# Second attention of a fused block on one core: rotation at later heads, score matmuls for one head at a time

## What is computed

```python
q, k, v = (proj(Wq), proj(Wk), proj(Wv))            # (b, H, s, d)
q, k = _rope(q, k, s, d, hidden_states.dtype)       # q*cos + _rotate_half(q)*sin, the same for k
scores = einsum('bhqd,bhkd->bhqk', q, k) / sqrt(d)
scores = maximum(scores + causal, neg)
tmp_sum = sum(softmax(scores, axis=-1), axis=-2)    # column sums
_, topk_idx = top_k(tmp_sum, int(0.1 * s))          # heavy columns
mask = heavy_mask[:, :, None, :] | band             # band: |i - j| <= 25
scores = where(mask, scores, neg)
attn = einsum('bhqk,bhkd->bhqd', softmax(scores, axis=-1), v)
return attn @ Wo.T
```

## Time and profile before

| | us |
|---|---|
| median of 3 runs | 2262.65 (2259.99 to 2265.01) |
| profiled execution | 2258.55 |
| its span in the trace | 2256.7 |
| PE, PEld busy | 2000.1, 1674.2 |
| DVE, ACT, POOL busy | 1312.0, 930.6, 219.9 |

### The profile page before, as it was taken

How to read it: one execution, slowest core, us unless ns; L and a number is a source line. 1 busy time by engine, 2 the same in 40 slices (tenths; PEclk the granted TensorE clock), 3 DMA queues, 4 the chain that set the end, 5 groups by cost and what they waited for, 6 DMA issues and landing times.

```text
span 2256.7 us, 84567 instructions
## 1 busy us (share of the span) xinstructions
PE 2000.1 (89%) x34605; PEld 1674.2 (74%) x34605; DVE 1312.0 (58%) x4974; ACT 930.6 (41%) x3362; POOL 219.9 (10%) x338
## 2 busy tenths in 40 slices
PE   5788888888889798866799999998999999999999
PEld 3455565565555677666789898998898988988987
DVE  3456465565576049755666666665666666666653
ACT  2253443543555122233444444443444444444432
POOL 0011011011011100000011011010110110110112
PEclk9789888899798898966899999999999999999999
DMA  6100000000000561200000000000000000000000
GB/s 248 31 6 16 19 6 15 16 10 15 17 8 2 194 231 56 88 3 17 18 17 4 27 18 18 13 18 19 27 4 18 27 4 27 18 18 13 4 12 10
DMA packets 61862, 74.95 MB, mean 33 GB/s; under 512 B 8480, under 2 KB 49888, under 8 KB 60608
## 3 DMA queue, kind: packets, MB, share of 16 engines
q1 hardware_dynamic: 59024, 54.82, 7.9%
q0 software_dynamic: 2448, 14.68, 1.9%
HBM read 44.27 MB, written 16.81 MB: 27 GB/s over the span
## 4 chain that ended last, share of the span: by engine, by line
PE 50%; DVE 5%; issue 2%; ACT 1%; DMA 0%; DVEq 0%; POOL 0%; ACTq 0%
PE ps L1374 26%; PE ps L1328 11%; PE ps L1308 10%; PE ps L1362 2%; PE ps L1317 1%; DVE hbuf L1544 1%; DVE dh L1532 1%; DVE dh L1538 1%; DVE cn L1522 0%; ACT nn L1441 0%; DVE hbuf L1541 0%; DVE cn L1510 0%; DVE hn L1525 0%; DVE h L1542 0%; DVE ns L1534 0%
## 5 line engine op out<-in xcount | busy, mean ns | idle before, releaser
L1374 PE MATMUL ps<-hbuf,whf 128*128 128x32 f16 x24480 | 657.9, 177 | 81.6 <-DVE hbuf L1544 59.0
L1374 PEld LDWEIGHTS ps<-hbuf,whf 128*128 128x128 f16 x24480 | 647.8, 96 | 104.2 <-DVE hbuf L1544 61.7
L1421 ACT ACTIVATE rz<-s,sc 128x32 f32<-128x32 f32 x512 | 164.5, 321 | 522.5 <-DVE s L1510 511.2
L1308 PE MATMUL ps<-hbuf,w1f 128*128 128x256 f16 x2304 | 292.7, 274 | 0.0
L1328 PE MATMUL ps<-hh,w2f 128*128 128x256 f16 x2304 | 292.1, 275 | 0.0
L1510 DVE TENSOR_REDUCE s<-ps 128x32 f32<-128x64 f32 x512 | 114.8, 224 | 273.4 <-PE ps L1374 260.0
L1497 POOL TENSOR_TENSOR hh<-tb,hh 128x256 f16<-128x256 f32 x192 | 132.4, 695 | 1302.1 <-ACT hh L1468 1302.1
L1308 PEld LDWEIGHTS ps<-hbuf,w1f 128*128 128x128 f16 x2304 | 224.1, 98 | 32.2 <-issue 6.0
L1328 PEld LDWEIGHTS ps<-hh,w2f 128*128 128x128 f16 x2304 | 211.4, 98 | 44.5 <-issue 19.9
L640 ACT ACTIVATE E<-ps,nm 128x128 f32<-128x128 f32 x256 | 94.9, 371 | 255.1 <-DVE nm L712 253.7
L1018 PE MATMUL ps<-x1T,wi 128*128 x768 | 173.9, 389 | 19.8 <-DMA wi<-in_W_ih 13.7
(11 more groups left out here) (192 smaller groups left out, 2824.6 us busy)
## 6 DMA issues: line engine op xcount, KB each, us to landing
gi_d<-stage SPq DMA_DIRECT2D x96, 128.0 KB, 1.7
gi<-gi_d SPq DMA_DIRECT2D x16, 768.0 KB, 5.1
swp<-raw SPq DMA_DIRECT2D x256, 32.0 KB, 1.9
w1f<-in_w1T POOLq DMA_DIRECT2D x4, 1408.0 KB, 9.0
xall<-in_x SPq DMA_DIRECT2D x4, 1024.0 KB, 9.0
x1T<-in_xT SPq DMA_DIRECT2D x1, 4096.0 KB, 22.0
w2f<-in_w2T POOLq DMA_DIRECT2D x2, 2048.0 KB, 10.5
out<-x1T SPq DMA_DIRECT2D x8, 512.0 KB, 3.1
```

The costliest lines, as they stand in the source:

```text
L1308: last = nc.tensor.matmul(ps[:, 6 + i % 2, 0:TT], w[:, wp, e % EH, c * P:(c + 1) * P], hbuf[par][:, k, hq, :, :].rearrange("p s b -> p (s ...
L1374: last = nc.tensor.matmul(ps[:, bank, g * WIDE * 2 * B:(g + 1) * WIDE * 2 * B], whp[:, k, w, q, g * P:(g + 1) * P], h[:, k, :, :].unsqueez ...
L1421: nc.scalar.activation(rz[:, q, :, :].rearrange("p g b -> p (g b)"), s1[:, q, :, :].rearrange("p g b -> p (g b)"), ACT.Sigmoid, scale=sc[: ...
```

## The change

The score matmuls are issued for one head at each head, and not for two at every other head; their wait for a free bank is written for one head (h - 4 where it was h - 3). The slots of the rotation are later by 3 for the first two units, by 5 for the third (which moves to round 1) and by 2 for the fourth. In batch 0 the swap of unit 1 is issued by ACT, between its second and its third copy; SP issues the other three.

```diff
@@ -406,24 +406,26 @@
+        def swap(queue, b, u):
+
+            i, p = UNITS[u]
+            x = raw[:, b % 2, i, 2 * p:2 * p + 2, :]
+            queue.wait_ge(a_raw, b * NU + u + 1)
+            passed(queue, v_rot, (b * NU + u - 1) * 3)
+            half = DH2 // 2
+            for to in range(0, P, half):
+                of = to + half if to % DH2 == 0 else to - half
+                queue.dma_start(swp[to:to + half, u % 2, :, :], x[of:of + half, :, :]).then_inc(d_swap[u % 2], 16)
...
-                for b in range(B):
+                swap(sp, 0, 0)
+                swap(sp, 0, 2)
+                swap(sp, 0, 3)
+                for b in range(1, B):
                     for u in range(NU):
-                        swap(b, u)
+                        swap(sp, b, u)
@@ -451,12 +453,12 @@
                     n = b * (2 * NH) + r * NH + h
-                    passed(pe, a_e, (n + 1 - 4 + 1) * 2)
+                    passed(pe, a_e, (n - 4 + 1) * 2)
...
-                    pair = [(g, g % 4, g // HPC, slice(g % HPC * DH2, (g % HPC + 1) * DH2)) for g in (h, h + 1)]
-                    for g, bank, m, rows in pair:
+                    heads = [(g, g % 4, g // HPC, slice(g % HPC * DH2, (g % HPC + 1) * DH2)) for g in (h,)]
+                    for g, bank, m, rows in heads:
...
@@ -574,8 +576,7 @@
                     for h in range(NH):
-                        if h % 2 == 0:
-                            scores(b, 0, h)
+                        scores(b, 0, h)
@@ -606,8 +607,7 @@
                     for h in range(NH):
-                        if h % 2 == 0:
-                            scores(b, 1, h)
+                        scores(b, 1, h)
@@ -671,6 +671,8 @@
                 for u in range(NU):
                     copy_raw(0, u, 4 + u)
+                    if u == 1:
+                        swap(act, 0, u)
@@ -831,7 +833,7 @@
-ROTATE_AT = (4, 5, 6, 7, 8, 9, 12, 13, 14, NH + 8, NH + 9, NH + 10)
+ROTATE_AT = (7, 8, 9, 10, 11, 12, NH + 1, NH + 2, NH + 3, NH + 10, NH + 11, NH + 12)
```

## The result

| | before | after |
|---|---|---|
| median, us | 2263.83 (2259.99 to 2267.33, 4 runs) | 2290.16 (2282.57 to 2293.45, 4 runs) |
| profiled execution, us | 2258.55 | 2282.57 |
| its span | 2256.7 | 2280.7 |

The ratio of the times is 1.0112, with a 95% interval of 1.0081 to 1.0143: the change makes the kernel slower by 1.1%, 26 us. The forecast was 2284 us, 21 more than before.

The account below looks back on a forecast made before the run. The second attention was taken as PE-bound, losing time to waits and half-speed clock. Start 0, middle cycles -7, last batch +14 and +14 made +21 us: median 2262.65 to 2284 us, range 2240 to 2320.

Parts of the forecast that it names:

- The cost of a single head: Score matmuls: without overlap two single heads cost 0.95 us more than a pair, 122 us of PE work, 15.2 a cycle.
- The rotation: Second attention: later slots remove almost all 14.0 us of DVE swap waits and 9.4 us of PE waits in a cycle.
- The middle cycles: Six cycles between heavy-column copies: 84.5 us each against 85.6, -7 for the six; 81.1 each without low clock.
- the third: Middle cycles: share of the earlier low clock assumed to stay, 8% of the time at 1.2 GHz.
- The start: Start and batch 0: DVE begins about 3 us earlier, against 7.6 us for eight pairs, over half taken up by waits; sum 0.
- The last batch: Last batch, no projections: +14 us for the stretch through its round 0, and +14 for round 1 at low clock.
- the term of 6.8 us: Round 0 of the last batch: heads 4 to 11 run at 1.2 GHz until the output projections, costing 6.8 us.
- The part behind the stage: Everything after the second attention: forecast change 0.
- A: Rival: PE, busy with hardly a gap, stays at 2.4 GHz throughout; -26 us, 2236; chance 0.15.
- B: Rival: clock falls in middle batches at heads 5 to 7 of round 0 and stays low; +32, 2316; chance 0.18.
- C: Rival: single heads still overlap, half of the 0.95 us paid; about -40 on the forecast, near 2244; chance 0.05.
- D: Rival: rotation still waits for swaps, 1 to 2 us a batch; within 5 us of forecast; forecast with D 0.57.

Follow-up runs that it names:

- products by head: Pairs with late rotation, each pair's products issued one head then the other, masks of both still ahead, against the kernel before: 2176.76 us, ratio 0.9624.
- wide fill: Changed kernel plus six useless full-width fp32 matmuls at each of heads 0 to 2, round 1, last batch: 2264.01 us, ratio 0.9992 to the kernel before.
- the first two experiments: Changed kernel with scores in pairs again, late rotation: 2179.64 us, ratio 0.9642; changed kernel with early rotation slots, single heads: 2329.85 us, ratio 1.0275.
- the narrow fill: Changed kernel plus four useless 32-row fp32 matmuls at each of heads 0 to 2, round 1, last batch: 2299.89 us, ratio 1.0159 to the kernel before.

## Why the prediction was right, and where it was not

The direction and the mechanism were right: twice the time for the products of two heads, the waits of DVE gone, a last round at 1.2 GHz. That the sum came so close was in part luck. Of its terms the start missed by -7.0 us, round 0 of the last batch and what stands ahead of it by -4.3, the last round by +5.7 and the part behind the stage by +7.8, and these cancel but for 2 us.

**The cost of a single head** was right. A head of round 0 takes 1.05 us (1.06 forecast), one of round 1 at 1.2 GHz 2.25 (2.25 forecast). The upper bound, no overlap at all, was the right one to take. PE's busy time in the stage grew by 95 us (578.1 to 673.3), over 80 as forecast. The experiment with products by head adds what the trace of before could not show: the order of the products does not separate the heads. That leaves the full-width masks, which are all that stands between two heads in the rows above.

**The rotation** was right for the middle cycles: PE's idle time fell by (76.7 - 12.4) / 6 = 10.7 us a cycle, 9.4 were forecast. (The swap was put at 6.3 us; its rows add up to 8 x 0.589 + 1.9 = 6.6. Nothing hangs on it.) DVE no longer waits for a swap in any of them; its 21.6 us of waits in the whole stage are the four swaps ahead of batch 0:

```profile
DVE swp L733 <- DMA swp<-raw: 21.6, 4, 12.6
```

What PE still waits for in the middle cycles is what the prediction kept, the diagonals and the output copy; no wait for `rdiag` or `En` is left there:

```profile
PE ps L468 <- POOL dg L438: 6.5, 6, 1.1
...
PE ps L486 <- ACT oT L664: 5.1, 6, 0.9
```

**The middle cycles** came out at 84.5 us, as summed: two of the six at 81.3 with a clock of 1.00, which is the sum without low clock (81.1), and the others longer by the low clock that they keep. The allowance of 8% of the time at 1.2 GHz is 8% in the row (0.96). That the mean agrees so well is in part luck: the third was a guess, and the cycles themselves go from 81.3 to 87.5.

**The start** was mis-sized: 0 forecast, -7.0 measured. The sum counted the swaps (-3) against the eight pairs (+7.6), but left out that the late rotation frees batch 0 from DVE's waits just as it frees the others. That is 10 to 11 us there by the experiments.

**The last batch** came out at +29.4 against +28 forecast, but not in the terms. Its round 0 stayed at 2.4 GHz from head 5 on, where I had put a price of 6.8 us for low clock: +9.7, not +14. In the two experiments with a fill in round 1, whose kernels are the same up to there, that round did fall to 1.2 GHz. The same cycle, in the run with wide fill, and its low stretch in round 0:

```profile
625.80:708.90 83.10, 82.00 (x487) 52.66 (x486) 45.59 (x172) 37.83 (x151) 9.67 (x16) 0.82 0.02 4
674.10:691.20 17.10, 17.10 (x70) 9.73 (x62) 5.62 (x27) 6.49 (x29) 0.00 (x0) 0.50 0.01 1
```

It takes 83.1 us, 11 more than in the changed kernel's trace; most of that is this stretch, the rest a longer low stretch in round 1 of batch 6. The run with single heads and early rotation falls there too. So the mechanism exists, the profiled execution missed it, and the term of 6.8 us is shown by the others. Round 1 was priced 5 us too low: the list of its work had 13 turns and 3 attends, but 16 and 4 stand before the output projections, 3 x 0.69 + 1.5 = 3.6 us, and the rest are the waits at the end, which low clock does not hide. At full clock the same list gave 29.5 us for the round; the run with wide fill took 36.2 - 4.2 = 32.0, short by the same turns and attend. The step that carried the term, that the clock falls behind the light columns and that nothing there brings it back, was right, and the two fills show that it hangs on the kind of work there and not on gaps between the matmuls.

**The part behind the stage** was put at nothing and took 7.8 us more in the profiled execution. Its instructions are the same, PE has 30331 in both. In the traces of the seven experiments it takes 1520 to 1531 us, with the same code, so there is a spread between executions of about the size of the 7.8. It goes with the clock: the changed kernel has 0.81 in 757 to 1100 us and 0.98 in the last 180.7, the kernel before 0.83 and 1.00 in about the same parts of the program. It may not be chance alone, however: in the four traces in which the clock is at 0.50 when the last output projections begin (the changed kernel, the first two experiments and the narrow fill) it takes 1530 to 1531 us, and in the other five 1520 to 1526.5; in the kernel before the clock falls just behind that point. No run tests this, and it is left open.

**The rivals.** A (the clock holds) is refuted by the narrow fill, and by the row from 698.8 us. The Trainium skill, page "TensorE: Matmul & The Clock Gate", section "What's actually happening", lets the gate go by how busy PE has been; read as busy time, this does not tell the two fills apart: PE was busy for 2.68 of 2.70 us with the narrow one and the clock fell, and with the wide one it stayed at 1.00. B (the clock low in the middle batches) happened in a small measure: the granted clock of the middle cycles lies between 0.92 and 1.00. C (1.05 us for a head) and D (no wait for a swap in the middle cycles) did not happen.

## What to carry to other kernels

In this kernel two small matmuls on different rows of the PE array ran in the time of one where nothing of full width stood between them, and did not where something did: put what they have in common (masks, first writes) ahead of both. When one engine waits for a DMA, ask which wait of PE stands behind it and what PE's clock does after that wait: here, with pairs, PE's idle time fell by 6.6 us a cycle and the cycle by 14. And a stretch of mostly narrow matmuls can be worth some wide work at its start, useful work if there is any: the last round took 53.1 us without it and 36.2 with it. It has to be measured: with pairs, where the clock fell less, no gain from such work is shown.

## What the runs showed of the hardware that was not expected

- A stretch with PE busy for 3.40 of 3.40 us, at 2.4 GHz and mostly on quarter rows, was followed by 51.2 us at 1.2 GHz. With 1.4 us of full-width fp32 work at each of three heads it stayed at 2.4 GHz; with fp32 work on 32 rows, 1.2 us in the first of them, it fell (2264.01 against 2299.89 us).
- The same instructions, from head 3 of the last round on, ran at 1.00 throughout in the run with wide fill and at 0.50 throughout in the changed kernel: here the level at which such a stretch began decided its time.
- Matmuls on different quarters of the rows start out of program order: with L475 of one head ahead of L473 of the other in the program, all passes of L473 start first, and the pair's products take 0.86 us, 0.85 in the other order. The Trainium skill, page "TensorE: Matmul & The Clock Gate", section "The mechanism", has matmuls start strictly in program order; the trace of this case shows another order of starts than the program has. It does not record the order in which PE was given them.
